# Two graph attention layers: source score rows by way of memory instead of TensorE, and the last head in plain order

## The reference, cut to what matters

```python
h = (x @ W).reshape(-1, H, C)                       # H = 4, C = 192
as_ = jnp.sum(h * a_src, axis=-1)                   # source scores: 1250 nodes x 4 heads
ad_ = jnp.sum(h * a_dst, axis=-1)                   # target scores
e = jax.nn.leaky_relu(as_[src] + ad_[dst], NEG_SLOPE)
m = jax.ops.segment_max(e, dst, num_segments=N)
e = jnp.exp(e - m[dst])
s = jax.ops.segment_sum(e, dst, num_segments=N)
out = jax.ops.segment_sum(h[src] * (e / s[dst])[:, :, None], dst, num_segments=N)
```

## Time and profile before

| what | value |
|---|---|
| median of 3 runs | 2639.05 (2638.74 to 2639.62) |
| profiled execution, its own time | 2642.76 |
| span of the profiled execution | 2641.0 |
| PE busy | 2567.0, 97% of the span |
| DVE busy | 1586.7, 60% |
| ACT busy | 779.6, 30% |
| DMA | 155.70 MB, mean 59 GB/s |

### The profile page before, as it was taken

The page is one execution under the profiler, slowest core; times in us unless marked ns, Lnnn a source line. Parts: engine busy times, 40 slices in busy tenths (PEclk is TensorE's granted clock), DMA queues, the critical chain, the costliest instruction groups (busy, mean ns, idle before and its releaser), DMA issues.

```text
span 2641.0 us, 26830 instructions
## 1 busy us (share of the span) xinstructions
PE 2567.0 (97%) x10673; PEld 1821.8 (69%) x10673; DVE 1586.7 (60%) x2708; ACT 779.6 (30%) x1314; POOL 347.4 (13%) x197
## 2 busy tenths in 40 slices
PE   7999999999999997999999999999999999999999
PEld 4667667558965987777777775465755786556676
DVE  4456471789948996997788998254432461341322
ACT  1043342016732873222222221430002431342000
POOL 0888888000000000000000000000000000000000
PEclk9999999999999998999999999999999999999999
DMA  9232313543020406000120002200350100213201
GB/s 255 23 46 14 50 2 49 142 124 104 20 60 0 106 11 214 1 0 1 72 100 2 24 24 85 99 1 0 97 182 18 36 0 1 59 35 131 86 24 59
DMA packets 138070, 155.70 MB, mean 59 GB/s; under 512 B 96524, under 2 KB 108390, under 8 KB 136418
## 3 DMA queue, kind: packets, MB, share of 16 engines
q1 hardware_dynamic: 67225, 153.56, 18.8%
q0 software_dynamic: 70720, 0.43, 2.8%
HBM read 117.75 MB, written 35.83 MB: 58 GB/s over the span
## 4 chain that ended last, share of the span: by engine, by line
PE 51%; DVE 7%; ACT 2%; issue 1%; DMA 0%; SPq 0%; DVEq 0%; ACTq 0%
PE psum L523 50%; DVE arena L1878 2%; DVE arena L1880 1%; DVE arena L1879 1%; PE psum L534 0%; DVE arena L1871 0%; ACT arena L1140 0%; ACT arena L1145 0%; ACT arena L1031 0%; DVE arena L1536 0%; DVE arena L1944 0%; DVE arena L1378 0%; DVE arena L1877 0%; DVE arena L1870 0%; DVE arena L1903 0%
## 5 line engine op out<-in xcount | busy, mean ns | idle before, releaser
L523 PE MATMUL psum<-arena 128*125 128x384 f32 (+12 forms) x9762 | 2459.8, 413 | 39.0 <-DMA arena<-in_ffn_w 7.1
L523 PEld LDWEIGHTS psum<-arena 128*125 128x125 f32 (+3 forms) x9762 | 1721.0, 188 | 751.5 <-issue 136.4
L2293 POOL DMA_INDIRECT count_matrix<-arena x170 | 342.8, 2016 | 122.8 <-DVE arena L1475 60.9
L1878 DVE RECIPROCAL arena<-arena 128x500 f32<-128x500 f32 x60 | 196.7, 3278 | 2.1
L1628 DVE CUSTOM_DVE_ANT_0 arena<-arena 125x1250 bf16<-125x1250 bf16 (+1 forms) x100 | 139.2, 1457 | 12.9 <-ACT arena L1173 12.3
L2303 POOL MEMSET arena<- 125x60 f32 x1 | 0.2, 207 | 1047.0 <-PE psum L523 1047.0
L1712 DVE TENSOR_TENSOR arena<-arena 125x1250 f32<-125x1250 f32 x80 | 116.3, 1453 | 18.5 <-ACT arena L1122 18.3
L1119 ACT ACTIVATE arena<-arena 125x1250 f32<-125x1250 f32 x80 | 106.9, 1336 | 54.5 <-PE psum L523 54.2
L1715 DVE SCALAR_TENSOR_TENSOR arena<-arena 125x1250 f32<-125x1250 f32 x80 | 116.9, 1461 | 2.8
L1031 ACT ACTIVATE arena<-psum 128x250 f32<-128x250 f32 (+1 forms) x102 | 40.6, 495 | 231.9 <-PE psum L534 231.5
L1265 ACT ACTIVATE arena<-psum,arena 128x250 f32<-128x250 f32 x120 | 49.3, 465 | 198.3 <-PE psum L523 198.3
(11 more groups left out here) (223 smaller groups left out, 1463.9 us busy)
## 6 DMA issues: line engine op xcount, KB each, us to landing
arena<-in_ffn_w SPq DMA_DIRECT2D x3, 4608.0 KB, 15.4
residual<-arena SPq DMA_DIRECT2D x30, 336.0 KB
arena<-residual SPq DMA_DIRECT2D x30, 336.0 KB
arena<-target_rows SPq DMA_DIRECT2D x12, 610.4 KB
arena<-in_gat_w SPq DMA_DIRECT2D x3, 2304.0 KB, 9.4
arena<-residual SPq DMA_DIRECT2D x10, 672.0 KB
residual<-arena SPq DMA_DIRECT2D x10, 672.0 KB
count_matrix<-arena SPq DMA_DIRECT2D x2, 3125.0 KB, 27.0
```

The costliest lines, as they stand in the source:

```text
L523: return pe.matmul(o, lhsT, rhs, start=start, stop=stop, skip_group_check=share)
L1878: now(dve.reciprocal(t_, t_))
L2293: pool.indirect_dma_start(counts[k], bass.IndirectOffsetOnAxis(ap=IDX_I[0:T, c:c + 1].bitcast(U32), axis=0), COUNT_I[0:T, c:c + 1], None, ...
```

## The change

Two things are done.

**Source rows through memory.** The 80 turns and 24 copies (`"asrow"` of layers 0 and 1) go. In layer 0 one transpose `("ast",)` turns all forty score columns at once into 40 rows of 125, ACT copies them to `AST`, and SP stores them to a new tensor `source_rows`. In layer 1 the four rows of `SCT` are stored there as they are, without a transpose. The new function `source_row(layer, h)` on SP reads one head's row back onto 125 partitions, into the buffers of before; for heads 2 and 3 it waits for the maxima of the head two before. DVE's first maximum of a head waits for this load instead of ACT's copy. In layer 1 ACT's first exponential waits until `SCT` is stored, since it writes over it.

**The last head in plain order.** `by_pairs` goes: all ten source tiles go through all five banks as in the other heads. The normalised tiles lie over `h`, so ACT now waits for the last bank ahead of the first `normalise`, where it waited ahead of the fourth.

```diff
@@ front
-            seq += {3: [("asrow", 3)], 4: [("rows", 0)], 5: [("step", 0)], 8: [("step", 1)]}.get(t, [])
+            seq += {4: [("rows", 0)], 5: [("step", 0)], 8: [("step", 1)]}.get(t, [])
...
-        seq += {0: [("turned_s", 0)], 1: [("asrow", 0), ("asrow", 1)], 8: [("asrow", 2)]}.get(t, [])
+        seq += {0: [("turned_s", 0)]}.get(t, [])
...
-ASROW_AFTER = {4: (0, 1), 8: (2,)}
@@ PE
             pe.wait_ge(a_drained, A_AT[("h", 0, NT - 1, 0)] + 1)
+            b = fill("A", ("ast",))
+            pe.transpose(b[0:H0 * NT, 0:T], ASC[0:T].rearrange("p a b -> p (a b)"), IDENT[0:T, 0:T]).then_inc(a_filled, 1)
...
-                    by_pairs = 4 if (layer, h) == (1, H0 - 1) else 0
-                    for j in range(NT - by_pairs):
+                    for j in range(NT):
...
-                    for b in range(5 if by_pairs else 0):
-                        for j in range(NT - by_pairs, NT):
...
@@ ACT
-                if stage == 1 and g == 3:
+                if stage == 1 and g == 0:
                     act.wait_ge(v_filled, V_AT[("acc", 1, H0 - 1, 4)] + 1)
...
+                if (layer, i) == (1, 0):
+                    act.wait_ge(as_saved, 32)
...
-            for h in range(H0 - 1):
-                asrow(0, h)
+            act.wait_ge(a_filled, A_AT[("ast",)] + 1)
+            act.activation(AST[0:H0 * NT], bank(("ast",))[0:H0 * NT, 0:T], ACT.Copy).then_inc(a_drained, 1)
@@ DVE
-                if t == 0:
+                if t == 0 and layer < 2:
+                    dve.wait_ge(asrow_loaded[h % 2], 16 * (2 * layer + h // 2 + 1))
+                elif t == 0:
                     dve.wait_ge(a_drained, A_AT[("asrow", layer, h, 2)] + 1)
@@ SP
+            def source_row(layer, h):
+                if h > 1:
+                    sp.wait_ge(max_done, layer * H0 + h - 1)
+                row = as_dram[layer, h * NT:(h + 1) * NT, :].rearrange("t q -> (t q)").rearrange("(o n) -> o n", o=1)
+                load(ASROWS[layer][h % 2][0:T], row.to_broadcast([T, N]), asrow_loaded[h % 2])
+
+            def beside_projection(t):
...
+                if t == 0:
+                    sp.wait_ge(a_drained, A_AT[("ast",)] + 1)
+                    load(as_dram[0], AST[0:H0 * NT], as_saved)
+                if t == 6:
+                    sp.wait_ge(as_saved, 16)
+                    sp.wait_ge(v_drained, V_AT[("mask", NT - 1, 2)] + 1)
+                    source_row(0, 0)
+                    source_row(0, 1)
+                if t == 9:
+                    source_row(0, 2)
...
+            residual(0, x, SLOT_M, res[XMID0], beside_projection, begun=True)
+            source_row(0, 3)
...
             row_load(0, "ffn0_b", frow_loaded)
+            sp.wait_ge(a_drained, A_AT[("s", 2)] + 1)
+            load(as_dram[1].rearrange("(a t) q -> a (t q)", a=H0), SCT[0:H0], as_saved)
+            sp.wait_ge(as_saved, 32)
+            for h in range(H0):
+                source_row(1, h)
             sp.wait_ge(max_done, 2 * H0)
```

More of the change, by code:

```diff
@@ L80, in front @@
         seq.append(("h", (t, 0)))
-        seq += {0: [("turned_s", 0)], 1: [("asrow", 0), ("asrow", 1)], 8: [("asrow", 2)]}.get(t, [])
+        seq += {0: [("turned_s", 0)]}.get(t, [])
     for t in range(NT):
         seq.append(("h", (t, 1)))
-        seq += {2: [("asrow", 3)], 4: [("rows", 0)], 5: [("step", 0)], 8: [("step", 1)]}.get(t, [])
+        seq += {4: [("rows", 0)], 5: [("step", 0)], 8: [("step", 1)]}.get(t, [])
     return seq
 COUNTS_BESIDE = {0: (3,), 1: (4,), 2: (5, 6), 3: (7, 8), 4: (9,)}
-ASROW_AFTER = {4: (0, 1), 8: (2,)}
 MAXIMA_AFTER = {5: 5, 6: 4, 7: 4, 8: 4, 9: 23}
@@ L153, in plan @@
     turned("mix0")
-    def asrow(h):
-        A.extend(("asrow", 0, h, q) for q in range(3))
     for t in range(NT):
         A.append(("h", 0, t, 0))
+    A.append(("ast",))
     for t in range(NT):
@@ L164, in plan @@
             V.append(("proj", t, half))
-        for h in ASROW_AFTER.get(t, ()):
-            asrow(h)
     gat(0)
@@ L219, in gps_kernel @@
     neg_dram = nc.dram_tensor("neg_saved", [T, NT * N], BF16).ap()
+    as_dram = nc.dram_tensor("source_rows", [2, H0 * NT, T], F32).ap()
     prow_dram = [nc.dram_tensor(f"target_rows{i}", [2, (H0 - 1) * NT, T], F32).ap() for i in range(2)]
@@ L307, in gps_kernel @@
         WA1S = small(KD, 2 * H0)
+        AST = mem(ROW_AT + 1000, T)
         PT = ROW[2][:, 0:2 * T].rearrange("p (a b) -> p a b", a=2)
@@ L467, in gps_kernel @@
         gatb_loaded, bc_loaded = sem("gat1_bias_loaded"), sem("gat0_bias_loaded")
+        as_saved, asrow_loaded = sem("source_rows_saved"), [sem(f"source_rows_loaded{i}") for i in range(2)]
         prow_saved, prow_turned = sem("target_rows_saved"), sem("target_rows_turned")
@@ L665, in _ @@
                     natural_product("V", ("proj", t, half), WP, HALF, AT, n0=half * HALF, tile=t)
-                if t == 4:
-                    pe.wait_ge(v_drained, V_AT[("mask", NT - 1, 2)] + 1)
-                for h in ASROW_AFTER.get(t, ()):
-                    column_rows(("asrow", 0, h), ASC[:, h, :])
             def gat_front(layer):
@@ L733, in gat4 @@
                             last.then_inc(et_used, 1)
-                    for b in range(5 if by_pairs else 0):
-                        for j in range(NT - by_pairs, NT):
-                            n = (layer * H0 + h) * NT + j
-                            if b == 0:
-                                pe.wait_ge(et_made, n + 1)
-                            for i in range(2):
-                                last = mm(banks[b][0:T, i * (C0 + 1):(i + 1) * (C0 + 1)],
-                                          ET4[n % 4][0:T, (2 * b + i) * T:(2 * b + i + 1) * T], hn(layer, j, h),
-                                          False, j == NT - 1, share=True)
-                        last.then_inc(v_filled, 1)
             def rows(layer, h, parts=range(2)):
@@ L1166, in asrow @@
             def asrow(layer, h):
-                if h > 1:
-                    act.wait_ge(max_done, layer * H0 + h - 1)
                 for q, (t0, n) in enumerate(TG):
@@ L2451, in _ @@
                 count_load(j)
-            def later_counts(t):
+            def source_row(layer, h):
[4 more added lines that the diff above has]
+            def beside_projection(t):
                 for j in COUNTS_BESIDE.get(t, ()):
                     count_load(j)
-            residual(0, x, SLOT_M, res[XMID0], later_counts, begun=True)
+                if t == 0:
[10 more added lines that the diff above has]
+            source_row(0, 3)
             sp.wait_ge(v_drained, V_AT[("mask", NT - 1, 2)] + 1)
```

## The result

| | before | changed |
|---|---|---|
| median of 6 runs each | 2639.34 (2638.74 to 2642.29) | 2630.59 (2625.16 to 2633.52) |
| ratio, 95% interval | | 0.9963 (0.9950 to 0.9975) |
| profiled execution, span | 2642.76, 2641.0 | 2630.19, 2628.4 |

What follows compares the result with a forecast made beforehand. PE, busy 97% of the span, was taken to bound the kernel, with DVE only 5.06 ahead in layer 0. Gains of 4.3 (layer 0), 5.1 (layer 1) and 1.0 (tail) sum to 10.4: median 2628.7, own range 2626 to 2632.

Steps and rivals of the forecast that it cites:

- Turns removed, 5.07 a layer: On PE in both layers: forty turns fewer in each layer take 5.07 from PE's time.
- Layer 0: the read-back comes in on DVE: Layer 0: first source row lands at 544.7, 0.5 late for DVE's maxima; layer 0 gains 5.07 - 0.8 = 4.3.
- The lower bound of the forecast, 1: Layer 0's least gain: both rows land together at 548.8, DVE 4.6 late, weights at 619.0, nothing but 0.4 left.
- the 0.3 kept for the mask's stores: Layer 0: risk allowance for DVE waiting on the mask's stores ahead of its first weights, at 611.9.
- Layer 1, 5.07: Layer 1: DVE has slack for the loaded rows, so the whole 5.07 is gained; bounds 4 and 5.1.
- The last head, 1.0: Tail: PE gains 8.4, but drains and normalisation become the path, leaving a gain of 1.0.
- the bound of 2.7: Tail's upper bound: clock high through the last head, each bank 1.7 earlier, gain 2.7.
- A: Layer 0's gain taken by DVE, rows landing together or mask's stores late: gains 0.4, sum 6.5, 2632.6; chance 0.15.
- B: PE turns cold in the tail's gap, slowing turns and later the FFN: tail -3.7, sum 5.7, 2633.4; chance 0.11.
- C: PE's clock stays high through the last head, tail 2.7, layer 0 whole: sum 12.9, 2626.2; chance 0.06.
- D: Source rows land 18 behind their issue instead of 6.5, delaying both layers: 7.5 slower, 2646.5; chance 0.04.
- E: PE's time isn't what counts, another chain reaches the same points: 2639; chance 0.04.

Runs made afterwards that it cites:

- k2_plain_only: The kernel before the change with only the last head put in plain order; 2639.26, ratio to before 0.9996.
- k5_warm: The changed kernel plus fifteen unread products of 193 columns on PE in the idle gap ahead of the last head's turns; 2630.80, ratio to before 0.9967.
- k1_rows_only: The changed kernel with the last head of layer 1 still bank by bank as before, so only source rows through memory; 2632.70, ratio to before 0.9970.
- k7_late1: The changed kernel with one additional load in layer 1, so its first source row lands later; 2631.39, ratio to before 0.9973.
- k10_warm0: The changed kernel plus five overwritten products of 193 columns on PE ahead of layer 0's first; 2630.32, ratio to before 0.9961.
- k4_pairs_of_two: The changed kernel with source tiles 8 and 9 of the last head going bank by bank; 2628.80, ratio to before 0.9958.
- k9_best: The changed kernel with rows in two pieces, head 0's row asked for one tile earlier, and last-head tiles 8 and 9 by pairs; 2626.07, ratio to before 0.9948.
- k3: The changed kernel with each source row read in two pieces, 112 and 13 partitions; 2627.66, ratio to before 0.9954.
- k6: The changed kernel with one additional load in layer 0, so its first source row is issued later; 2635.22, ratio to before 0.9988.

## Why the prediction held, and where not

**Turns removed, 5.07 a layer.** Right. PE's own way in layer 0 is shorter by 5.07 when nothing else holds it. In layer 1 it was 5.6: there the turns cut the `h` products into four pieces that took 55.2, and in one piece they take 54.45. I had priced only the turns. In layer 0, where the turns cut the row of products too, no such gain showed, so what makes it stays open.

**Layer 0: the read-back comes in on DVE.** The mechanism was right, the size off. I took 0.8 of the 5.07 away; it was 1.63. The step is "I take 544.7, the nearest row: 0.5 later than 544.23": against `k2_plain_only`, whose first maximum stands 64.91 behind the mark, it came 1.5 later (66.42). It took 8.3 from its issue, not 7.2. (The 3.4 that the prediction sets against its sum, from the Trainium skill's page "DMA: Bandwidth & Descriptors", section "Anatomy of one DMA", is a fit for DMAs issued by POOL; this row is issued by SP, so the 8.3 says nothing against the page.) The size was also a matter of the execution: with the same code `k5_warm` landed in 7.5 and had layer 0's products 4.2 sooner, at full clock, close to the 4.3 forecast, and `k1_rows_only` landed in 9.9. Why the landing differs so was not looked into; that the two rows share their engines may be part of it. (The lower bound of the forecast, 1, does not fit the 0.4 that its own sentence gives.) From the first maximum to the first weights every kernel here took 70.13 to 70.17, so the 0.3 kept for the mask's stores was not needed: they ended in time.

**A term that was missing.** PE's wait of 2.04 lowered the clock behind it, 1.65. The earlier trace rows had shown this for the tail, and the forecast used it there, but layer 0's wait was priced at its own length. Such a wait of PE costs its length and what the clock does after it.

**Layer 1, 5.07.** Right in kind; the rows have slack, shown by `k7_late1`. The first maximum came 22.5 behind the first score product, where 780.4 would have meant 23.2.

**The last head, 1.0.** Under-sized: 2.4, near the bound of 2.7. The step that failed is the time at which the banks are full. I placed the plain order's products at the times of before and so kept the low clock that followed the wait of 1.89 at the head's start (62 products in 22.17, in `k1_rows_only` 21.23). In the changed kernel the clock fell one head earlier, at 919.90, the wait at the last head's start was 0.96, and it stayed at 1.00 behind it. So the products end 137.7 behind layer 1's start and not 138.7; the first normalised pair follows 2.0 earlier than before, where 0.8 was forecast. At which head's start the clock falls is not the change's doing: in `k10_warm0`, with the same code and the fall at the last head, the products end at 139.0 and the tail gains 0.9, close to the 1.0 forecast. The spacing of the normalised pairs is that of DVE and ACT, as forecast (2.47 for 2.5). On ACT:

```profile
989.90 1.94 ACT L1034 ACTIVATE arena<-arena 125x768 f32<-125x768 f32 x2 [0.92 <-DVE arena L1376]
992.37 1.94 ACT L1034 ACTIVATE arena<-arena 125x768 f32<-125x768 f32 x2 [0.43 <-DVE arena L1376]
```

**Rivals.** A's mechanism, DVE as the later one, was at work, but cost 1.6 where A had 4.7. B's first half is refuted: the first turns went cold, but they lay hidden; by the time of the second group (2.84) the clock was back. Its second half, a later return of the clock in the FFN, happened in small. In stretches of 1.0 from the FFN's first product the clock is 0.50 in the first three and 0.59 in the fourth before, and 0.50 in the first four and 0.70 in the fifth after; the FFN's first run of products takes 592.11 and 592.50. C came true in the tail and not in layer 0. D and E are out: the first row landed 7.5 to 9.9 behind its issue, where D had 18, and layer 0 followed the row one to one.

**Sum.** 9.2 in the stages against 10.4, 8.75 in the medians. The errors of layer 0 (-2.5) and of layer 1 and the tail (+1.9) mostly cancelled, so that the median came this close is in part luck. Of the -0.6 from the FFN on, 0.4 is the clock that came back later there. In all eleven profiled executions that run of products takes 591.97 to 593.26, and `k4_pairs_of_two` and `k9_best`, which end the last head alike, are 1.3 apart; so one execution of each kernel does not show that the change is to blame.

## What to carry to other kernels

When a transfer replaces work on the engine that bounds, look at how many DMA engines it can use: a row read onto 125 partitions went through 5 of 16, and 112 + 13 was worth about 3 more (3.3 in the profiled stage, 3.6 in the medians' gains, whose intervals overlap). What can be taken from the bounding engine is at most the lead of the next one (here DVE's 5.06), less what the new load takes from that lead; and how long a load takes to land differs from one execution to the next (here 7.5 to 9.9), so a forecast that uses up such a lead has to carry that spread. And a short wait of PE, of a size that looks harmless, is to be priced with the clock after it, unless another wait follows that takes it up.

## What the runs showed of the hardware

PE's wait ahead of layer 0's products, and the time of these 400, in eleven profiled executions (clock in the stretches behind the start):

| kernel | wait | 400 products |
|---|---|---|
| before, `k2`, `k3`, `k9` | 0.36 to 0.37 | 131.29 to 131.31 |
| `k10` (filled) | 0.36 | 131.3 |
| `k6`, `k5` | 0.68, 1.22 | 131.27, 131.27 |
| changed, `k4`, `k7` | 2.04, 2.21, 2.35 | 132.95, 132.93, 132.94 |
| `k1` | 2.52 | 134.24 |

In the slower ones the granted clock fell to its lower level (0.50) for a few microseconds behind the wait; in the others it stayed at 1.00. It isn't the wait alone that decides. In layer 1 PE waits 1.89 ahead of the third head; behind that the clock fell in nine executions, but not in `before` and `k10`, which waited 1.89 ahead of the last head as well and fell there. Behind a wait of 2.66 the first turns of the tail took 4.32 in `k4` and 2.78 in `k9`. Behind one of 2.85 near 146, in code that all share, the same run of products took 40.19 in `k6`, 41.88 in before and 43.21 in `k5`. What else decides was not tried. Such falls, 0.9 to 3.0 each where they were measured above, are large enough to make up a good part of the spread of the changed kernel's runs (2625.16 to 2633.52); that they do was not tested.

Source rows read onto 125 partitions ran at a DMA share of 0.30; read onto 112 and 13, for the same bytes on each partition, the share was 0.78 in the same stretch.

From its issue the first row of layer 0 landed in 8.3 in the changed kernel, 9.9 in `k1`, 8.6 in `k4` and `k7`, 7.5 in `k5` and 7.7 in `k10`, all with the same code up to there, and in 6.5 in two pieces (`k3`).
